# A recommender kernel on one core: fp32 work in smaller pieces, the score table placed in eight chunks, the mask built on VectorE

## The reference

```python
ub = concatenate([table_i1[his[:, :, 0]], table_i2[his[:, :, 1]], table_i3[his[:, :, 2]]], axis=2)
mask = his[:, :, 0] == 0
att_in = concatenate([q, ub, q - ub, q * ub], axis=-1)        # q: the candidate item, broadcast
score = where(mask, 0.0, ((att_in @ w_att1.T + b_att1) @ w_att2.T + b_att2)[..., 0])
browse = einsum('bl,ble->be', score, ub)
feat = concatenate([item_emb, browse, user_emb], axis=-1)
x = dice(feat @ w1.T + b1); x = dice(x @ w2.T + b2); out = sigmoid(x @ w3.T + b3)
```

## Time and profile before

| | |
|---|---|
| median of 3 runs (lowest, highest) | 1651.27 us (1649.88, 1658.23) |
| the profiled execution, and its span | 1650.01 us, 1648.2 us |
| TensorE busy, share of the span | 1485.0 us, 90% |
| VectorE | 1454.9 us, 88% |
| ScalarE | 1193.0 us, 72% |
| GpSimd | 1270.7 us, 77% |
| mean granted TensorE clock, share of 2.4 GHz | 0.960 |

### The profile page before, as it was taken

How to read it: one execution, slowest core, us unless ns; L and a number is a source line. 1 busy time by engine, 2 the same in 40 slices (tenths; PEclk the granted TensorE clock), 3 DMA queues, 4 the chain that set the end, 5 groups by cost and what they waited for, 6 DMA issues and landing times. The chain is left out here.

```text
span 1648.2 us, 76679 instructions
## 1 busy us (share of the span) xinstructions
PE 1485.0 (90%) x31007; PEld 1377.5 (84%) x31007; DVE 1454.9 (88%) x1514; ACT 1193.0 (72%) x1921; POOL 1270.7 (77%) x1988
## 2 busy tenths in 40 slices
PE   4898989899898989989799998989999898998965
PEld 3788989899898989989798898989889898988861
DVE  6699898989989899998889989898998989899955
ACT  5586767778677777867678786777868777785636
POOL 3588787877878788787778878787887878787850
PEclk8799999999999999999899999999999999998976
DMA  2112020111202011120201102021120202111000
GB/s 42 51 43 67 25 76 24 54 46 36 73 21 80 24 54 46 39 70 22 79 24 50 51 26 82 19 65 42 46 54 27 82 18 64 42 48 47 23 22 0
DMA packets 33023, 74.45 MB, mean 45 GB/s; under 512 B 15471, under 2 KB 20463, under 8 KB 28911
## 3 DMA queue, kind: packets, MB, share of 16 engines
q1 hardware_dynamic: 25656, 68.48, 14.4%
q0 software_dynamic: 2144, 1.36, 0.8%
q10 hardware_dynamic: 4952, 0.28, 0.2%
HBM read 7.02 MB, written 0.01 MB: 4 GB/s over the span
## 5 line engine op out<-in xcount | busy, mean ns | idle before, releaser
L552 PE MATMUL wsum_ps<-scaled_lo,onehot_hi 100*128 100x75 bf16 x12288 | 550.0, 201 | 99.6 <-DVE scaled_lo L990 91.5
L552 PEld LDWEIGHTS wsum_ps<-scaled_lo,onehot_hi 100*128 100x128 bf16 x12288 | 500.4, 99 | 130.0 <-DVE scaled_lo L990 117.3
L759 ACT ACTIVATE hiT<-hiT_ps 128x800 bf16<-128x800 bf16 x512 | 430.4, 841 | 193.7 <-PE hiT_ps L516 184.6
L990 DVE TENSOR_TENSOR scaled_lo<-onehot_lo,parts 100x3744 bf16<-100x3744 bf16 x256 | 546.6, 2135 | 21.0 <-POOL parts L426 14.8
L538 PEld LDWEIGHTS sel<-scoretab,hiT 128*128 128x128 bf16 x12288 | 496.1, 99 | 68.9 <-issue 35.4
L538 PE MATMUL sel<-scoretab,hiT 128*128 128x75 bf16 x12288 | 533.0, 201 | 17.9 <-DMA scoretab<-scores_b 12.3
L978 DVE TENSOR_REDUCE score_j<-sel 100x24 f32<-100x600 f32 x512 | 395.9, 773 | 124.6 <-PE sel L538 123.3
L767 ACT ACTIVATE wsum_ring<-wsum_ps 128x300 f32<-128x300 f32 x512 | 361.1, 705 | 195.8 <-PE wsum_ps L552 169.7
L412 POOL TENSOR_TENSOR score<-score_j 100x16 f32<-100x16 f32 x256 | 196.6, 768 | 190.8 <-DVE score_j L978 187.4
L415 POOL TENSOR_TENSOR score<-score,score_j 100x16 f32<-100x16 f32 x256 | 321.4, 1256 | 20.1
L946 DVE TENSOR_TENSOR onehot_hi<-digits,iota_hi 100x1920 bf16<-100x1920 bf16 x256 | 300.4, 1174 | 2.9 <-PE wsum_ps L552 2.9
(11 more groups left out here) (158 smaller groups left out, 1024.0 us busy)
## 6 DMA issues: line engine op xcount, KB each, us to landing
scoretab<-scores_b SPq DMA_DIRECT2D x96, 375.0 KB
weightsum<-wsum_ring SPq DMA_DIRECT2D x128, 125.0 KB
weightsum<-wsum_ring SPq DMA_DIRECT2D x64, 150.0 KB
raw<-in_r_rec_his_dram SPq DMA_DIRECT2D x32, 150.0 KB, 4.0
item_rows<-in_L_rec_table_i_dram,ids_now POOLq DMA_INDIRECT x51
table_blk<-in_L_rec_table_i_dram SPq DMA_DIRECT2D x3, 125.0 KB
user_rows<-in_L_rec_table_user_dram,ids_now POOLq DMA_INDIRECT x16, 3.5
weightsum<-in_L_rec_w_dram ACTq DMA_DIRECT2D x6, 25.0 KB
```

Source lines behind the costliest of these rows:

```text
L552: mm = pe.matmul(wsum_ps[:, b * W:(b + 1) * W].rearrange("p (j v) -> p j v", j=NF), hi_columns(n % 4, g), scaled_lo[:, n % 2, g, i % 3, :] ...
L759: act.activation(hiT[:, s % 2, 0:8 * POS], hiT_ps[:, 0:8 * POS], ACT.Copy).then_inc(hiT_copied, 1)
L990: ins = dve.tensor_tensor(scaled_lo[:, n % 2, :, :, :].rearrange("p q i (u d) -> p (q i) u d", d=2), onehot_lo[:, n % 2, :, :, :].rearrang ...
```

## The change

- `finish` is spread over 11 slots, 7 to 17 (`PARTS` = 11), in parts of two or three matmuls; `layer1` moves to slot 18, `userT` to 19.
- Stage 0 of a four-block round is cut in two pieces, "first" and "rest", in two slots. With them the table takes 25 slots, 4 to 28, instead of 21.
- In a slot TensorE's piece stands ahead of `add_scores`; ScalarE's order stays.
- `place_scores` moves an eighth of a tile (16 users) at a time, with a semaphore for each; `read_scores` waits for its chunk in every fourth slot, `split_copy` for all eight before the table is overwritten. The order in SyncE's queue changes.
- `make_keep` moves from GpSimd to VectorE, in steps 5 and 13.

```diff
-        PARTS = 6
+        PARTS = 11
-                 FIN_SLOT + PARTS: "layer1", 16: "userT", 20: ("digit", 1, 0), 21: ("digit", 0, 0)}
+                 FIN_SLOT + PARTS: "layer1", 19: "userT", 20: ("digit", 1, 0), 21: ("digit", 0, 0)}
-        SPLIT_SLOT = 3
+        CHUNK = TILE // 8
+        split_at = {}
+        for r, (l0, l1) in enumerate(ROUNDS):
+            for piece in ("first", "rest", 1, 2) if l1 - l0 == 4 else ("all", 1, 2):
+                split_at[4 + len(split_at)] = (r, piece)
+        SPLIT_DONE = 3 * NR
...
+            def place_scores(t, c):
+
+                await_ge(split_copied, SPLIT_DONE * (t + 1))
+                if isinstance(t, int) and t == 0:
+                    sp.wait_ge(scoretab_zero, c // 4 + 1)
                 else:
-                    await_ge(sel_full, SLOTS * t - (16 if hb == 0 else 0))
+
+                    await_ge(sel_full, SLOTS * t - (SLOTS - 4 * c - 4))
+                hb, rows = c // 4, slice(c % 4 * CHUNK, (c % 4 + 1) * CHUNK)
                 for j in range(NF):
                     r = slice(hi_first(j), hi_first(j) + HI)
+                    sp.dma_start(scoretab[r, hb, j, rows, :, :].rearrange("p b k v -> p (b k v)"),
+                                 scores_b[r, c * CHUNK:(c + 1) * CHUNK, :, :].rearrange("p b k v -> p (b k v)")
+                                 ).then_inc(scoretab_in[c], 16)
...
             def tile(t, last=False):
-                place_scores(t, 1)
+                for c in range(4, 8):
+                    place_scores(t, c)
...
                 collect_sums(t, 1)
+                collect_sums(t, 2)
                 if not last:
-                    place_scores(t + 1, 0)
-                collect_sums(t, 2)
+                    for c in range(4):
+                        place_scores(t + 1, c)
...
-                if s in (0, 16):
-
-                    pe.wait_ge(scoretab_in, (2 * t + s // 16 + 1) * (NF * 16))
+                if s % 4 == 0:
+
+                    pe.wait_ge(scoretab_in[s // 4], (t + 1) * (NF * 16))
...
+            def split_piece(r, piece, copied, first=False):
+
                 o = split_bank(first, r)
                 l0, l1 = ROUNDS[r]
+                if piece in (1, 2):
+                    await_ge(split_copied, copied)
+                    mm = pe.matmul(o, minus_identb[:, :], scores_b[:, :, piece - 1, l0:l1], start=False,
+                                   stop=(piece == 2), skip_group_check=True)
+                else:
+                    if piece != "rest" and not (isinstance(copied, int) and copied == 0):
+                        await_ge(split_copied, copied)
+                    mid = (l0 + l1) // 2
+                    for lo in range(mid if piece == "rest" else l0, mid if piece == "first" else l1):
+                        mm = pe.matmul(o[:, :, lo - l0], tableT[:, lo, :], queryT[:, :], start=(lo == l0), stop=False,
                                        skip_group_check=True)
+                if piece != "first":
+                    mm.then_inc(split_full, 1)
...
+                if s in split_at and not last:
+                    r, piece = split_at[s]
+                    if r == 0 and piece == "first":
+
+                        await_ge(task_copied, task_before(t, 1) + 1)
+                    split_piece(r, piece, SPLIT_DONE * (t + 1) + (3 * r + (piece if piece in (1, 2) else 0)))
                 if s >= LAG:
                     add_scores(t, s - LAG)
...
+                    if r == 0 and stage == 0:
+
+                        for c in range(8):
+                            act.wait_ge(scoretab_in[c], (t + 1) * (NF * 16))
+                    split_copy(r, stage, SPLIT_DONE * (t + 1) + (3 * r + stage + 1))
...
+            def make_keep(t, hb):
+
+                if isinstance(t, int) and t == 0 and hb == 0:
+                    dve.wait_ge(task_copied, DIGITS0)
+                else:
+                    dve.wait_ge(task_copied, task_before(t, 3) + 1 if hb else tasks_start(t))
+                if not (isinstance(t, int) and t == 0):
+                    dve.wait_ge(parts_ready, (t - 1) * STEPS + 8 * hb + 8)
+                d = [digits[:, hb, k, :, NF - 1, 0] for k in range(2)]
+                dve.tensor_tensor(keep[:, hb, :], d[0], d[1], ALU.add).then_inc(keep_step, 1)
+                dve.wait_ge(keep_step, 2 * t + hb + 1)
+                dve.tensor_scalar(keep[:, hb, :], keep[:, hb, :], -float(MID), None, ALU.is_gt
+                                  ).then_inc(keep_ready, 1)
...
                 pick(t, 2 * n + 1)
+                if n == 5:
+                    make_keep(t, 1)
+                if n == 13 and not last:
+                    make_keep(t + 1, 0)
```

More of the change, by code:

```diff
@@ L175, in build @@
         scoretab_clear = sem("scoretab_clear")
-        scoretab_in = sem("scoretab_in")
+        scoretab_in = [sem(f"scoretab_in{c}") for c in range(8)]
         weightsum_in = sem("weightsum_in")
@@ L334, in tile @@
                 collect_sums(t, 1)
+                collect_sums(t, 2)
                 if not last:
-                    place_scores(t + 1, 0)
-                collect_sums(t, 2)
+                    for c in range(4):
+                        place_scores(t + 1, c)
             load_rows(1)
-            place_scores(0, 0)
+            for c in range(4):
+                place_scores(0, c)
             tile(0)
@@ L442, in step @@
                     gather_users(t, 2 * t + (3 if last else 4))
-                if n == 5:
-                    await_ge(task_copied, task_before(t, 3) + 1)
-                    make_keep(2 * t + 1, 1)
-                if n == 12 and not last:
-                    await_ge(task_copied, task_before(t, 21) + 1)
-                    make_keep(2 * t + 2, 0)
             chain(pool.memset(identf[:, :], 0.0))
@@ L677, in slot @@
                     add_scores(t - 1, s - LAG + SLOTS)
-                i = s - SPLIT_SLOT
-                if 0 <= i < 3 * NR and not last:
-                    if i == 0:
-                        await_ge(task_copied, task_before(t, 1) + 1)
-                    split_stage(i // 3, i % 3, 3 * NR * (t + 1) + i)
             pe.wait_ge(const_ready, 1)
@@ L696, in _ @@
                         pe.wait_ge(const_ready, 2)
-                    split_stage(r, stage, NR * (stage - 1) + r + 1 if stage else 0, first=True)
+                    split_piece(r, stage if stage else "all", NR * (stage - 1) + r + 1 if stage else 0, first=True)
             transpose_hi(0, 0)
@@ L873, in slot @@
                     copy_sums(t - 1, s - LAG + SLOTS)
-                i = s - SPLIT_SLOT
-                if 0 <= i < 3 * NR and not last:
-                    if i == 0:
-                        act.wait_ge(scoretab_in, (2 * t + 2) * (NF * 16))
-                    split_copy(i // 3, i % 3, 3 * NR * (t + 1) + i + 1)
+                if s in split_at and split_at[s][1] != "first" and not last:
+                    r, piece = split_at[s]
+                    stage = piece if piece in (1, 2) else 0
+                    if r == 0 and stage == 0:
+                        for c in range(8):
+                            act.wait_ge(scoretab_in[c], (t + 1) * (NF * 16))
+                    split_copy(r, stage, SPLIT_DONE * (t + 1) + (3 * r + stage + 1))
             act.wait_ge(blk_zero, 2)
```

32 lines of the change are left out of this document (3 added, 29 removed).

## The result

| | before | after |
|---|---|---|
| median of 12 runs each | 1651.62 us | 1642.19 us |
| lowest and highest | 1645.23, 1659.55 | 1637.62, 1646.60 |
| profiled execution, its span | 1650.01, 1648.2 us | 1637.62, 1635.8 us |
| mean granted TensorE clock | 0.960 | 0.975 |
| ratio of the times (95% interval) | | 0.994 (0.9917 to 0.9962) |

The change saves 9.4 us of the medians (12.4 between the two profiled executions), and the interval leaves out 1. Forecast were 24: the direction was right, the time is inside the range (1597 to 1660), the size was not.

What follows compares the result with a forecast made beforehand. Bound by TensorE's fp32 humps, then VectorE (5.30 us a step), then a step 15 stall. Gains of 17 us in 14 tiles, 4.5 start, 2.5 first and last tile: 24 off 1650 gives 1626, median 1627; own range 1610-1640, eight-in-ten 1597-1660.

Steps and rivals of the forecast that it cites:

- The turn: TensorE and ScalarE, slots with a subtracting piece: add_scores, copy of sums, piece's copy, piece take 2.82 us, against 2.42 without.
- Rival C: Slots with the TensorE-ScalarE loop: it is 0.15 us longer in some 14 slots, 2.1 us a tile, 1656 us; chance 0.12.
- Rival A: Loop through ScalarE does not bind: tile 93.1 us, time 1598 us, median 1600; chance 0.14.
- The lead: Per tile: engines carry work ahead between steps, 0.9 us in the old kernel; 0.5 (0 to 0.9) taken off, giving 95.1.
- The plain sum: Changed tile: steps 3 to 13 68.46, steps 14 and 15 5.54 + 5.69, steps 0 to 2 15.90; 95.59 us.
- Start: Before tile 0: TensorE's 9.56 us wait for half a table shrinks, 4 to 7 us gained, 4.5 taken.
- First and last tile: First tile loses its hump of tables, last its finish slots of 3.0 us: 2.5 us gained together, 0 to 5.
- Mask: VectorE, steps 5 and 13: two operations per half cost 0.5 us (0.2 to 0.8), hidden; GpSimd's 0.91 us parts wait goes.
- Rival B: Tile's end: the stall in step 15 stays, 1.9 us a tile, 27 us back, 1654 us; chance 0.13.
- Rival D: SyncE's queue of table transfers is late above 0.83 us per issue; at 1.0, 57 us more, 1684 us; chance 0.13.
- the 53 us of one by one: Table transfers: served one by one, 24 x 2.2 = 53 us a tile would not fit in 27; judged unlikely.
- The eight waits of ScalarE: ScalarE's waits in slot 5 for the table chunks cost 8 x 0.03 = 0.25 us in slot 6 (0 to 0.8).

Runs made afterwards that it cites:

- the kernel with the copies turned: Changed kernel with only ScalarE's order altered, split_copy ahead of copy_sums in a slot: 1602.73 us, ratio 0.9699 to the kernel before.
- the second execution: Both kernels run and profiled once more, unchanged: medians 1651.09 us (before) and 1645.08 us (changed).
- both repairs at once: Changed kernel with TensorE's piece behind add_scores again and ScalarE's split_copy ahead of copy_sums: 1653.38 us, ratio 1.0012 to the kernel before.
- piece behind: Changed kernel with one thing undone, TensorE's table piece behind add_scores again: 1618.94 us, ratio 0.979 to the kernel before.

## Why the forecast was right in its parts and wrong in its sum

**The turn: right.** Forecast 2.82 us with 0.06 for the signal, measured 2.84 with 0.14 for it and shorter links elsewhere. Steps 3 to 13 were forecast at 68.46 in sum; in tile 5 they are 68.62 (95.80 less 5.60, 5.18, 5.72, 5.25 and 5.43), and no step is off by more than 0.18. Slot 22 took 3.36 against 3.42, and the longest wait before a piece is the 0.9 that was forecast near 1. Rival C is refuted. Rival A is the kernel with the copies turned: its tile of 93.1 and time of 1600 stand against 93.43 and 1602.7. The forecast even had the order's cost in it, 2.0 us a tile between A and the sum, and the runs say 2.4.

**The lead, -0.5 a tile: the step that failed.** The plain sum was 95.59 and the tile is 95.80. I took 0.5 off because the same sum for the kernel before came out 0.9 too high, and credited the changed kernel with the same effect; no row of the changed kernel's own work stood behind it. The prediction doesn't list its sum for the old kernel step by step, but the steps of that kernel show where it can have been ahead (steps 2, 8, 11 and 12 of tile 5):

```profile
537.54:542.36 4.82, 4.82 (x117) 4.50 (x115) 4.82 (x6) 4.69 (x9) 3.75 (x8) 1.00 0.29 87
...
576.88:581.94 5.06, 5.06 (x118) 4.52 (x116) 5.06 (x6) 4.42 (x9) 4.16 (x7) 1.00 0.14 34
...
593.41:598.61 5.20, 5.00 (x117) 4.45 (x115) 5.04 (x7) 5.16 (x11) 3.96 (x8) 1.00 0.01 3
598.61:603.66 5.05, 4.60 (x113) 4.31 (x113) 5.05 (x6) 4.00 (x7) 4.22 (x6) 1.00 0.30 74
```

All four are shorter than VectorE's 5.30; together they fall short of it by 1.07 us. By the bare 5.30 of VectorE, a step can be that short only where VectorE had got ahead, while TensorE worked off a hump or a stall. In the changed kernel only steps 1 and 14 are below 5.30, by 0.12 and 0.05. That the lead came from the humps is read from these steps; no run tested it by itself. The change levels the humps, which is one reason why the correction did not carry over. The turn is a second: the kernel with the copies turned has the same levelled work, its step 12 is 4.77, and the plain sum for it (A's 93.1 with the 0.5 put back, 93.6) is 0.2 above its tile of 93.43, while with the turn it is 0.2 below. The runs don't part the two. With 14 tiles the 0.5 is 7 us of the error; 0.2 a tile in the sum itself is another 3. Likewise the end: steps 14 and 15 came out at 10.68 against 11.23, and steps 0 to 2 at 16.50 against 15.90. The five together are 27.18 against 27.13.

**Start and first tile.** Start: forecast -4.5, measured -5.4, of the 9.56 us between the transfers' issue and the first `read_scores` 4.1 are left (4.1 again in the second execution). First and last tile: forecast -2.5, measured +1.7 and -0.5. In both kernels TensorE runs at half clock until near 60 us, so a tile that starts 5.4 us earlier has 5.4 us more of itself in that stretch. That cover was in the page and I gave it no price. The steps of tile 0 bear it out: steps 0 to 2 take 18.64 us before and 21.02 after, the other thirteen 0.65 less. And in the kernel with both repairs at once (1653 us), which starts tile 0 at 41.2 too but has its clock back at 50.4 us instead of 60.0, steps 0 to 2 take 17.74. The end behind the last tile gave 1.3, and that isn't the change: from the start of the last step to the end of the span it is 67.48 us before and 66.04 after here, and 67.50 and 67.25 in the second executions.

**The account.** -5.4 + 1.7 - 6.8 (14 tiles; a typical one 96.40 to 95.83 by the medians) - 0.5 - 1.3 makes -12.3, the spans' -12.4; the other 3 us up to the medians' -9.4 are the difference between executions. How large that is, the second pair of profiles shows: their spans are 5.7 apart (1645.4 and 1639.7), with a start only 2.1 us earlier.

**Mask: right.** 0.5 per half, as measured (0.32, 0.23, less an overlap), and hidden. Its worth, 11 to 13 us, was measured in both kernels, but how it divides between the wait and the low clock was not: in the old kernel the 0.91 us wait went away, and 7 low clocks in 14 tiles stayed. That VectorE would no longer wait for `parts` was wrong: it does, 16.1 us in 20 places, all but one now in slots 7 to 10, where TensorE binds.

**Rival B, low clock in step 15: refuted for this kernel**, 5.43 us at 1.00. But what cured it is not what I said. The mask alone left it in 7 of 14 tiles (0.77 in step 14 of tile 5). It went in the kernels in which splitting pieces reach slot 28 and the table lands in time, which may be because TensorE stays fed: in the changed kernel TensorE is busy 4.83 us of 5.25 in step 14. But with `finish` spread alone, and nothing of the splitting work behind slot 23, the clock of step 15 is 1.00 as well (6.79 us, 4.52 busy, 1.98 idle at a stretch). So what tips the clock at a tile's end was not isolated and stays open.

**Rival D, the queue: refuted.** 24 transfers took 18.52 us at the start, 0.77 each (forecast 0.78); in tile 5, with SyncE's waits for the slots that read the old table, 19.98 us, which is the 0.83 each from which D was to decide, and still TensorE never waits for `weightsum` in a tile of the loop: the 1.2 us to spare were counted too tightly. The rule of the Trainium skill (DMA: Bandwidth & Descriptors, section Bandwidth) is to batch to at least 1 MiB for 75% of the peak bandwidth; the 2 us of fixed cost, which the prediction names with it, stand in another section of the same page of the Trainium skill, on the anatomy of a DMA, for transfers issued from GpSimd. Here a transfer has 94 KB, and from the first issue to the first use 4.1 us pass; but the issues follow each other in 0.77 us, so they overlap, the 53 us of one by one didn't come, and the eight pieces alone made no difference that can be told (1653.33 us). The eight waits of ScalarE that I priced at 0.25 cost nothing to speak of: from the sums' copy to the table's in slot 6 it is 0.51.

**What I did not see at all** is that the eight table pieces are what makes the finer splitting possible. I had priced them for the start only. Without them the later end of the table costs 2.9 us a tile.

## What to carry to other kernels

Where two in-order engines hand two kinds of work to each other in each slot, write both in the same order on both engines; opposite orders close a loop through both queues, here 2.84 us against 2.4 in a slot, worth 39 us (copies turned) or 23 us (piece behind) with everything else alike. A sum over steps that uses the old kernel's carried lead as a correction must ask whether the change removes the unevenness that made the lead, or adds a coupling that uses it up. And parts tried alone can mislead in both directions: two that cost 22 and bring nothing gained 23 together, and two that bring 12 each added 10 in all to that pair.

## What the runs showed of the hardware

- The granted clock was at half when tile 0 began, in all fifteen profiles. It fell between 32.6 and 39.5 us and came back between 50.4 and 66.8 us, near 60 in the kernels before and after alike, whose tile 0 began at 46 and 41 us: an earlier start there is partly run at half speed.
- TensorE idle for 1.49 us in a stretch of light work (4.52 us busy in the 5.50 before) was followed by half clock, and the same 24 matmuls lasted 1.53 instead of 1.05 us; 1.32 us idle in the earlier trace rows was not. But the length of the idle time doesn't decide alone: 1.97 us in step 15 of the kernel before was followed by half clock (0.80), 1.98 us in the same step with `finish` spread was not (1.00).
- The same kernel started its first tile at 40.8 in one execution and at 44.5 in another, with 0.57 of the clock in the prologue of the second (20 to 28 us) and 1.00 in that of the first.
- From the end of a ScalarE copy to the start of the TensorE instruction that waits for it: 0.14 us (598.51 to 598.65), from VectorE 0.06 by my earlier reading.
